# A static schedule whose planner may also choose the engine: bank copies, sums and weightings placed one by one, and weighted values in pairs

## The reference

```
h   = norm(x) * (1 + scale[b]) + shift[b]          # scale, shift from the conditioning vector
att = softmax(q @ k.T / sqrt(d)) @ v               # 16 heads; q, k, v from h (cross: k, v from the context)
x   = x + gate * (att @ wo + bo)                   # gate in layer 3 only
x   = x + gate * (act(h @ w1 + b1) @ w2 + b2)      # feed-forward blocks
```

## Time and profile before

| | us |
|---|---|
| median of 3 runs (1527.33 to 1531.53) | 1530.13 |
| the profiled execution | 1532.15 |
| its span, first to last instruction | 1530.1 |
| mean granted TensorE clock, share of full speed | 0.983 |
| PE busy | 1417.4 (93%) |
| DVE busy | 1282.2 (84%) |
| ACT busy | 1139.8 (74%) |
| POOL busy | 931.0 (61%) |
| chain that ended last: PE, DVE, ACT, POOL | 57%, 26%, 11%, 4% |

### The profile page before, as it was taken

One profiled execution on the slowest core, in us unless ns is written; L12 is line 12 of the kernel. 1 busy time (PEld: TensorE's weight loads), 2 busy tenths in 40 slices (PEclk: granted clock), 3 DMA queues, 4 the chain that ended last, 5 costly groups with the idle time before them and its releaser, 6 DMA issues.

```text
span 1530.1 us, 40756 instructions
## 1 busy us (share of the span) xinstructions
PE 1417.4 (93%) x15176; PEld 1173.9 (77%) x15176; DVE 1282.2 (84%) x3592; ACT 1139.8 (74%) x4878; POOL 931.0 (61%) x1060
## 2 busy tenths in 40 slices
PE   5999999999989999899999999999899999999977
PEld 4887877977868878788778877877777878788745
DVE  6878888687899978888799988988888787988886
ACT  0658879878878587978787776777877788878764
POOL 4667656455577665665566656686566554745563
PEclk9999999999999999999999999999999999999988
DMA  9300000000000000000000000000000000000000
GB/s 279 125 2 2 2 1 2 2 1 2 8 8 1 8 6 4 1 2 2 1 8 6 4 8 2 8 6 3 6 4 2 2 2 2 2 3 2 3 3 6
DMA packets 15221, 20.65 MB, mean 13 GB/s; under 512 B 4400, under 2 KB 11568, under 8 KB 15024
## 3 DMA queue, kind: packets, MB, share of 16 engines
q1 hardware_dynamic: 13616, 14.44, 3.1%
q10 hardware_dynamic: 1408, 3.61, 0.7%
HBM read 16.99 MB, written 1.05 MB: 12 GB/s over the span
## 4 chain that ended last, share of the span: by engine, by line
PE 57%; DVE 26%; ACT 11%; POOL 4%; issue 1%; DMA 1%; SPq 0%; ACTq 0%; DVEq 0%; POOLq 0%
PE ps L776 11%; PE ps L900 10%; ACT E L989 9%; DVE negmax L1274 8%; PE ps L940 6%; PE ps L926 5%; PE ps L792 5%; PE ps L802 4%; DVE E L1391 3%; PE ps L863 3%; PE ps L951 3%; PE ps L877 3%; POOL E L1117 2%; PE ps L913 2%; DVE E L1340 2%; PE ps L890 2%
## 5 line engine op out<-in xcount | busy, mean ns | idle before, releaser
L989 ACT ACTIVATE E<-ps,negmax 128x128 f32<-128x128 f32 x2048 | 726.5, 423 | 102.0 <-DVE negmax L1274 96.4
L1117 POOL TENSOR_TENSOR E<-E,rinv 128x512 f32<-128x512 f32 x512 | 530.4, 1048 | 291.2 <-DVE rinv L1283 288.2
L989 ACT ACTIVATION_READ_ACCUMULATOR E<-ps,negmax 128x1 f32 x2048 | 533.8, 263 | 0.0
L1274 DVE TENSOR_REDUCE negmax<-ps 128x4 f32<-128x512 f32 x512 | 324.9, 679 | 39.9 <-PE ps L863 17.6
L900 PE MATMUL ps<-consts,E 128*128 128x128 f32 x2048 | 295.4, 280 | 32.0 <-POOL E L1117 20.4
L900 PEld LDWEIGHTS ps<-consts,E 128*128 128x128 f32 x2048 | 232.0, 143 | 89.3 <-POOL E L1117 54.2
L1391 DVE COPY E<-ps 128x512 f32<-128x512 f32 x384 | 254.0, 680 | 35.3 <-PE ps L900 32.8
L1110 POOL TENSOR_TENSOR E<-E,prod 128x512 f32<-128x512 f32 x128 | 162.1, 1273 | 51.3 <-DVE prod L1343 48.3
L998 ACT ACTIVATE VV<-ps 128x512 f32<-128x512 f32 x128 | 77.3, 624 | 103.8 <-PE ps L792 103.6
L1056 POOL TENSOR_TENSOR rstd<-ve,consts 128x1 f32<-128x1 f32 (+1 forms) x192 | 107.6, 564 | 69.0 <-DVE ve L1227 62.9
L926 PEld LDWEIGHTS ps<-E,VV 128*64 128x64 f32 x2048 | 111.8, 138 | 26.3 <-issue 4.9
(11 more groups left out here) (143 smaller groups left out, 2663.9 us busy)
## 6 DMA issues: line engine op xcount, KB each, us to landing
w_f<-res_f SPq DMA_DIRECT2D x6, 256.0 KB, 9.6
E<-in_x SPq DMA_DIRECT2D x16, 64.0 KB, 1.8
w_cq<-res_cq SPq DMA_DIRECT2D x2, 512.0 KB, 8.6
w_co<-res_co SPq DMA_DIRECT2D x2, 512.0 KB, 11.2
w_f<-res_f SPq DMA_DIRECT2D x2, 512.0 KB, 8.5
out_x<-X SPq DMA_DIRECT2D x16, 64.0 KB, 1.5
E<-in_ctx SPq DMA_DIRECT2D x16, 48.0 KB, 2.2
w_ck<-res_ck SPq DMA_DIRECT2D x2, 384.0 KB, 10.1
```

Source lines behind the costliest of these rows:

```text
L989: last = nc.scalar.activation(E[p][:, h, :], bank(u, j * N, (j + 1) * N), ACT.Exp, bias=negmax[p][:, h:h + 1], accum_out=sums[p][:, h:h + 1])
L1117: tt(e, e, rinv[p][:, T4 * g:T4 * g + T4].unsqueeze(2).broadcast_to([N, T4, N]), ALU.mult).then_inc(done[POOL], 1)
L1274: nc.vector.tensor_reduce(negmax[p][:, T4 * g:T4 * g + T4], bank(u).rearrange("p (h m) -> p h m", h=T4), AX, ALU.max, negate=True).then_in ...
```

## The change

1. `takers(key)` gives the engines that may run a step, with assumed durations, and the planner keeps one of them. `PT`, `O`, wide `V` and flat `Q`, `K` copies, `T`, `CT` and `PV` may go to VectorE or ScalarE; `prob`, the rotary sums and `xb` to GpSimd or VectorE. `schedule()` returns where each was placed (`PLACED`), and both engines have code for each.
2. Moved steps of VectorE with SBUF operands are among those that wait for the port in the plan.
3. `MX` takes two groups in one step: `MX0` and `MX1` in place of `MX0` to `MX3`, same products.
4. New numbers for `AGE`, `TURN`, `AHEAD` (none for rope any more), `LEAN`, `FAVOUR`, `KEEP` and the assumed arrival of the first loads.
5. The inputs of stream 1 are issued by ScalarE ahead of the weights, and ScalarE waits for the inputs of stream 0 before it issues `lnc` and the weights.

```diff
+def takers(key):
+    _, step, b, _ = key
+    if step[:4] == "prob" or step in SUMS or step == "xb":
+        return {POOL: 1.0, DVE: 0.6} if step[:4] == "prob" else {POOL: 0.41, DVE: 0.2} if step == "xb" else {POOL: 1.236, DVE: 0.6}
+    if step[:2] == "PT" or step[0] == "O" or KIND[b] in ("rope", "flat") and step in ("V0", "V1") \
+            or KIND[b] == "flat" and step in GROUP:
+        return {DVE: 0.6, ACTE: 0.48}
+    return {DVE: 0.32, ACTE: 0.25} if step in ("T", "CT") else {DVE: 0.24, ACTE: 0.25} if step == "PV" else {}
...
-        if k == "small":
-            add(PE, f"MX{g}", 0.242, (e, f"PT{g}"), (DVE, "V"), *([(PE, f"MX{g - 1}")] if g else []),
-                fills=() if g else ("PV",))
+        add(DVE, f"PT{g}", 0.6, (PE, f"PT{g}"), empties=f"PT{g}")
+        if k == "small" and g % 2:
+            add(PE, f"MX{g // 2}", 0.484, (DVE, f"PT{g - 1}"), (DVE, f"PT{g}"), (DVE, "V"),
+                *([(PE, "MX0")] if g > 1 else []), fills=() if g > 1 else ("PV",))
...
     return key[0] == DVE and (key[1] in ("norm", "squares", "factors", "heads", "keys")
-                             or key[1] == "sum" and key[2] >= L3_SELF)
+                             or key[1] == "sum" and key[2] >= L3_SELF) or key[1][:4] == "prob" or key[1] in (*SUMS, "xb")
...
     def make_ready(key):
-        e = key[0]
-        known[key] = max([end[a] + (SIGHT[e] if a[0] != e else OWN_RESULT if e != PE else -1e9)
-                          for a in after[key]] + [arrival(key)])
-        ready[e].append(key)
+        for e in cost_on[key]:
+            known[key, e] = max([end[a] + (SIGHT[e] if placed[a] != e else OWN_RESULT if e != PE else -1e9)
+                                 for a in after[key]] + [arrival(key)])
+            ready[e].append(key)
...
-                    for j in range(T4):
-                        q0 = 32 * j
-                        last = mm(ps[q0:q0 + 32, u[0], 0:N], vmask[p][:, r, q0:q0 + 32], E[p][:, T4 * r + j, :],
-                                  start=(r == 0), stop=(r == 3), tile_position=(0, q0))
+                    for r in (2 * i, 2 * i + 1):
+                        for j in range(T4):
+                            q0 = 32 * j
+                            last = mm(ps[q0:q0 + 32, u[0], 0:N], vmask[p][:, r, q0:q0 + 32], E[p][:, T4 * r + j, :],
+                                      start=(r == 0), stop=(r == 3), tile_position=(0, q0))
...
+                elif step[:4] == "prob":
+                    g = int(step[4])
+                    count = DONE[DVE, f"rcp{g}", b, s]
+                    if fresh(dve, done[DVE], count):
+                        dve.wait_ge(done[DVE], count)
+                    e = E[p][:, T4 * g:T4 * g + T4, :]
+                    tt(e, e, rinv[p][:, T4 * g:T4 * g + T4].unsqueeze(2).broadcast_to([N, T4, N]),
+                       ALU.mult).then_inc(done[DVE], 1)
...
             load(0)
             sp.dma_start(V[:, :], vecs).then_inc(vecs_loaded, 16)
             sp.dma_start(R[:, 0:D], rows[0:D].partition_broadcast(128)).then_inc(row_first_loaded, 16)
-            load(1)
...
             act.dma_start(stage["mod_first"], setup_w["mod_first"]).then_inc(mod_first_loaded, 16)
+            act.dma_start(xin[1], x[1]).then_inc(x_loaded[1], 16)
+            act.dma_start(cin[1], ctx[1]).then_inc(x_loaded[1], 16)
+            act.wait_ge(x_loaded[0], 32)
             act.dma_start(LNC[:, :], lnc).then_inc(lnc_loaded, 16)
```

More of the change, by code:

```diff
@@ L55 @@
 LEAVE_TILED = {"row32": 0.1, "row64": 0.1, "col32": 0.114, "col64": 0.151}
[L58 to L63, removed]
+AGE = 14.8
+TURN = [0, 0, 0, -4, -4, 2, 5, -3, 7, 1, 0, -3, 0, -8, 13, 24]
+AHEAD = {"small": 9.3, "flat": 4.8}
+LEAN = {PE: 0.00172, DVE: 0.0, ACTE: 0.0, POOL: 0.0}
 FAVOUR = {
[L67 to L82, removed]
@@ L85 @@
-KEEP = {
[L86 to L90, removed]
+    (POOL, "RK", "rope"): -4, (POOL, "gb", "small"): 96, (POOL, "power", "flat"): -2, (POOL, "power", "rope"): 40,
@@ new lines @@
+    (POOL, "power", "small"): -2, (POOL, "prob", "rope"): -152, (POOL, "xb", "ff"): -56, (POOL, "xb", "small"): 8,
+    (POOL, "zero", "small"): -10, (ACTE, "O", "flat"): 30, (ACTE, "O", "rope"): -2, (ACTE, "U0", "ff"): 20,
+    (ACTE, "U1", "ff"): 56, (ACTE, "V", "flat"): 4, (ACTE, "exp", "flat"): -22, (ACTE, "exp", "rope"): -92,
+    (ACTE, "exp", "small"): -20, (PE, "FOLD", "small"): 48, (PE, "G", "small"): -64, (PE, "K", "rope"): -20,
+    (PE, "MX", "small"): -12, (PE, "O", "flat"): -2, (PE, "O", "rope"): -20, (PE, "PJ", "rope"): -6,
@@ new lines @@
+    (DVE, "Q", "flat"): 86, (DVE, "T", "ff"): 62, (DVE, "T", "flat"): -4, (DVE, "T", "rope"): 20,
+    (DVE, "T", "small"): 26, (DVE, "U1", "ff"): 10, (DVE, "V", "small"): 2, (DVE, "VAR", "small"): -4,
+    (DVE, "aggr", "flat"): 24, (DVE, "aggr", "rope"): -92, (DVE, "aggr", "small"): -2, (DVE, "heads", "small"): -4,
+    (DVE, "max", "small"): -34, (DVE, "norm", "ff"): 6, (DVE, "norm", "rope"): -12, (DVE, "rcp", "rope"): -14,
+    (DVE, "rcp", "small"): 40, (DVE, "squares", "small"): 140, (DVE, "stats", "rope"): -134,
@@ L226, in steps_of @@
     return out
[L229 to L240, removed]
+SUMS = ("RQ0", "RK0", "RQ1", "RK1")
+def takers(key):
[6 more added lines that the diff above has]
+    return {DVE: 0.32, ACTE: 0.25} if step in ("T", "CT") else {DVE: 0.24, ACTE: 0.25} if step == "PV" else {}
 def table_of(key):
@@ L248, in table_of, with tail_of @@
     return {2: "gelu", 5: "gelu_tanh", 8: "gelu"}.get(b, "exp")
-def tail_of(key):
-    engine, step, b, _ = key
+def tail_of(key, engine):
+    _, step, b, _ = key
     if engine == PE:
@@ L406, in schedule @@
             for key in ready[e]:
[L407 removed]
+                t, n = known[key, e], len(fills[key])
                 if n:
@@ L412, in schedule @@
                         t = max(t, vacant[open_[n - 1]] + SIGHT[PE])
-                if turning[key] and turned >= 2:
-                    if turned - 2 >= len(added):
+                if turning[key] and len(turned) >= 2:
+                    if turned[-2] not in end:
                         continue
-                    t = max(t, added[turned - 2] + SIGHT[DVE])
+                    t = max(t, end[turned[-2]] + SIGHT[DVE])
                 if ahead[key] is not None:
@@ L428, in schedule @@
                 if best is None or score < best[0]:
-                    best = (score, key, start, open_[:n])
+                    best = (score, key, start, open_[:n], e)
             if best is not None and (choice is None or best[2] < choice[2]):
                 choice = best
[L432 to L436, removed]
+        _, key, start, banks, e = choice
+        for taker in cost_on[key]:
+            ready[taker].remove(key)
+        placed[key] = e
+        free[e] = clock.run(start, cost[key]) if e == PE else start + cost_on[key][e]
+        end[key] = free[e] + tail_of(key, e)
         order[e].append(key)
@@ L453, in schedule @@
                 make_ready(user)
-    return order, bank_of, fills, max(end.values())
-ORDER, BANK_OF, FILLS, MODELLED = schedule()
+    return order, bank_of, fills, placed, max(end.values())
+ORDER, BANK_OF, FILLS, PLACED, MODELLED = schedule()
 UNIT, _turns = {}, [0] * BANKS
@@ L475 @@
 for _b, _s, _n in UNIT:
-    _last = {"PV": "MX3", "PJ": "PJ" if KIND[_b] == "small" else "PJ1"}.get(_n)
+    _last = {"PV": "MX1", "PJ": "PJ" if KIND[_b] == "small" else "PJ1"}.get(_n)
     _fill = next(_key for _key in ORDER[PE] if _key[2:] == (_b, _s) and (_key[1] == _last or _n in FILLS[_key] and not _last))
@@ L902, in step_of @@
                 elif step[:2] == "MX":
-                    r = int(step[2])
-                    for by, count in latest_first((DVE, DONE[DVE, "V", b, s]), EMPTY[UNIT[b, s, f"PT{r}"]]):
+                    i = int(step[2])
+                    for by, count in latest_first((DVE, DONE[DVE, "V", b, s]), *[EMPTY[UNIT[b, s, f"PT{2 * i + n}"]] for n in (0, 1)]):
                         if fresh(pe, done[by], count):
```

138 lines of the change are left out of this document (103 added, 35 removed).

## The result

The changed kernel takes 1468.96 us (median of four), the kernel before 1528.73 beside it: ratio 0.9605, 95% interval 0.9582 to 0.9628. Three of its four runs lie from 1467.77 to 1469.30 (median 1468.62); the fourth took 3092.72 us, is left out of the ratio, and is explained by nothing here.

A forecast was written before the change was run, and what follows sets the result against it. TensorE, 93% busy, was taken as the bound. Pairs -6, middle -15, head -5 and tail -3 gave -29 us, from 1532.15 to 1503 (1501 in the median's terms); 8-in-10 range 1472 to 1542, the forecast's own 1482 to 1520.

The forecast's parts named there:

- The middle: TensorE's 73.7 us idle between head and tail: a fifth filled, -15 us; ends -45 and +20.
- the choice that I had called even: Copies and narrow steps on VectorE or ScalarE: durations about equal, so the swap is even; steps find the free engine.
- The new favours: New favours, banks kept back and ages change only the order; no term, within the middle's ends of -45 and +20.
- The clock: TensorE's granted clock, 0.99 in the middle, 0.88 at the end: follows the stalls, no cause of its own; no term.
- The pairs, -6: `MX` in double steps: about 92 runs on the 32-column tiling, 26 fewer at 0.235 us, -6 us; ends -14, +2.
- The head, -5: Reordered first loads: first projection at 12.4 us, 5.8 earlier, sign before 13.5; -5 us kept, ends 0 and -8.
- The tail, -3: Last 80 us: some ten chain weightings on VectorE, each 0.36 us shorter, -3 us; ends 0 and -8.
- The moved steps: About 125 weightings and sums (ends 40 and 250) go from GpSimd to VectorE; copies move to ScalarE.
- The lock: VectorE instructions with two SBUF inputs and GpSimd's weightings exclude each other; every moved step is exposed.
- rival A: The lock decides, slower: moved steps meet GpSimd in 68 of 125 cases, 1548 us in the median's terms; chance 0.15.
- Rival B: No gain in the middle; only head, tail and switches remain in part, about -8, 1522 us; chance 0.17.
- rival C: Large gain: middle -37, 75 runs of `MX` (-10), head and tail -6 each, -59, 1471 us; chance 0.13.

The follow-up runs named there:

- fit_nonarrow: Changed kernel with `T`, `CT`, `PV` on VectorE, choice left for wide copies, weightings and sums, numbers fitted anew: 1478.85 us, ratio 0.9650.
- fit_all: Changed kernel with all its choices, only its numbers searched further, with the same effort as the other fitted kernels: 1471.44 us, ratio 0.9612.
- fit_nonesingle: Changed kernel without choice of engine and without pairs, new loads kept, numbers fitted anew: 1499.61 us, ratio 0.9793.
- fit_single: Changed kernel with its choices but weighted values one group at a time (MX0 to MX3), numbers fitted anew: 1482.20 us, ratio 0.9686.
- fit_none: Changed kernel without any choice of engine, pairs and loads kept, numbers fitted anew: 1499.21 us, ratio 0.9799.
- b_head: Kernel before, plan unchanged, with the changed kernel's loads of the start: 1526.03 us, ratio 0.9959.
- head_old: Changed kernel, plan unchanged, with the loads of the start as they were before: 1473.06 us, ratio 0.9612.
- r_none: Changed kernel planned anew without choice of engine; its numbers, not fitted to that rule, pairs and loads kept: 1534.99 us, ratio 1.0026.
- f_wide: Changed kernel, plan kept as an order, every wide copy back on the engine of the kernel before: 1579.76 us, ratio 1.0327.

## Why the prediction was wrong, step by step

**The bound** was right: TensorE went from 93% to 95%, and the gain came out of its idle time, its switches and its clock.

**The middle, "I take a fifth of it, -15 us"**, is the step that failed, by its size. Idle there fell by 35 us, inside the end of -45 that I had written down, but I had drawn the fifth from one releaser, GpSimd's weighting. That wait did fall, by 14.2 us over the whole span (20.4 to 6.2), but the greater part of the 35 came out of the many other small waits. Two causes share it. One is the choice that I had called even: copies and narrow steps are worth 23 us in the fitted kernels, the weightings 5. An even swap of durations says nothing of the wait before it. In the changed kernel ScalarE waits 73.3 us for TensorE before 49 of its 108 `T` (the row of L1010), that is, it often stood ready when the bank came. It takes them although its 0.472 us is longer than VectorE's 0.401 (L1321): the planner goes by the earliest start, and its assumed durations (0.25 and 0.32) have the order the wrong way round. Most of the 23 seems to lie in the wide copies, since fit_nonarrow, without the choice for the narrow steps, is only 7 us above fit_all. The other cause is the next step.

**"The new favours ... change only the order; ... they lie within these ends"** failed with it. The new fit alone is worth some 25 us with no choice and no pairs (fit_nonesingle's idle is 83.4 us against 112.7), and a change of 1 in twelve numbers costs 34. I gave this edit no term. The file could have said so before any run: `MODELLED` is 1467.6 in the kernel before and 1421.4 in the changed one, 46 us less. That is nearer to the measured 60 than my 29, and I did not read it.

**The clock, "it follows the stalls and is no cause of its own"**: if so, it had to be in the sum. About 13 us of passes came back with it, nearly as much as my whole term for the middle.

**The pairs, -6**: 83 visits against my 92, and 9.9 us less in the products' row. As a cause it is shown only beside the choice (fit_single, 11 us); in the kernel before it bought nothing, and fit_none is no faster than fit_nonesingle. "Nobody waits long for `PV`" was the wrong cover to ask for: the loss was on TensorE, where the single step had filled waits.

**The head, -5**: first projection 4.3 us earlier (forecast 5.8; the sign asked for less than 13.5 us, it was 13.88), TensorE's idle in the first 20 us 4.3 less, and b_head -5.5 us. So it was right in the kernel before. In the changed kernel it is not shown to reach the end: head_old moved by 1 us, within its error.

**The tail, -3**: not seen. TensorE idles 18.8 of the last 76 us, where it idled 18.6 of the last 76 before (57.43 busy from 1454 to 1530).

**The moved steps**: 79, within 40 to 250 but not 125, and wide copies went the other way, to VectorE.

**The lock** is there, and costs little in this plan. The longest weighting of VectorE, in order of time in the changed kernel, began just as GpSimd started its second:

```profile
1248.40 2.03 POOL L1146 TENSOR_TENSOR E<-E,rinv 128x512 f32<-128x512 f32 x2
...
1249.44 1.54 DVE L1391 TENSOR_TENSOR E<-E,rinv 128x512 f32<-128x512 f32 x1
```

But the means are 0.734 on VectorE (median 0.692) and 1.055 on GpSimd (1.048 before), far from the 1.0 and 1.10 that I had set for rival A. The plan counts VectorE's side; whether that is why it stayed so cheap was not tested. Rival B fell too; rival C, 1471 us with over half of the middle's idle, 75 runs and 6 us at each end, is nearest to what came, at a chance of 0.13. Its term for the middle was right (37 for 35); that its total came out as well is luck, since the clock was missing in it and the tail (0.6 us) and the head were too large.

## What to carry to other kernels

When every engine runs a fixed list, an even swap between two engines is not worth nothing: price it by the waits that it can fill, not by the two durations. A plan fitted by search must be compared with another that was fitted as long; undoing one part inside a fitted plan measures the break (110 us for the wide copies), not the part (the whole choice for copies and narrow steps is worth 23). Where the file computes a finish of its own, read it before forecasting: here its differences from the kernel before came within 15 us of the measured ones for every plan made anew but r_none (21 us off). And put the clock into the sum: here 41 us less idle came with some 13 us of passes back at full speed. It is no fixed rate. f_wide idles 152 us, 40 more than the kernel before, and its mean clock is 0.985 against 0.983.

## What the runs showed of the hardware that I had not expected

A plan as an order on four engines repeats within 0.4% on one chip (0.1 to 0.4% between the lowest and highest run of each experiment), although moving twelve small numbers by one changes its time by 2 to 3%. The mean granted clock does not follow from the amount of TensorE's idle time alone: fit_none and fit_nonesingle idle 88 and 83 us and have 0.987 and 0.993. ScalarE's modulated copy with two operands a partition (scale and bias) takes 0.472 us in the mean (median 0.457, 0.443 to 0.713) on 128 x 128, more than the 0.394 and 0.405 of the copy with a bias alone (L1013 before, L1039 after; medians 0.368 and 0.393), so that VectorE, at 0.401, is the faster of the two for this step.
